# Ten scatters, then six: the row scatters of each batch split around the next inverse transform

## The reference, cut to what matters

```
u = x @ W_in + b_in
uc = _short_conv(u, short_w, short_b)          # three taps
x0, x1, v = split(uc, 3)
v = v * x1
v = _causal_fft_conv(v, k, filter_bias)        # k from a small sine network
y = v * x0
x = layernorm(x + y @ W_out + b_out)
probs = softmax(x @ gate_w.T);  top_w, top_idx = top_k(probs, 4)
act = silu(x @ w1) * (x @ w3);  eout = act @ w2          # for the 4 chosen experts
x = layernorm(x + sum(top_w * eout) + shared(x))
```

## Time and profile before

| | us |
|---|---|
| median of 3 runs | 703.61 |
| lowest, highest | 697.77, 704.76 |
| the profiled execution | 701.09 |
| its span in the trace | 699.3 |
| PE busy | 585.7 (84%) |
| DVE busy | 477.2 (68%) |
| ACT busy | 347.9 (50%) |
| POOL busy | 373.0 (53%) |

### The profile page before, as it was taken

The page is one execution under the profiler, slowest core; times in us unless marked ns, Lnnn a source line. Parts: engine busy times, 40 slices in busy tenths (PEclk is TensorE's granted clock), DMA queues, the critical chain, the costliest instruction groups (busy, mean ns, idle before and its releaser), DMA issues.

```text
span 699.3 us, 11663 instructions
## 1 busy us (share of the span) xinstructions
PE 585.7 (84%) x3264; PEld 504.2 (72%) x3265; DVE 477.2 (68%) x1108; ACT 347.9 (50%) x698; POOL 373.0 (53%) x341
## 2 busy tenths in 40 slices
PE   5795989989798997989857668898888999888853
PEld 3685868768587785877635568797787889788843
DVE  5869798949678696877956654444444459787835
ACT  3643456656367563666226134444444456465623
POOL 0535152756827568373647745554555547556561
PEclk9897999989899897998896589899999999999986
DMA  7395111633313232223847336664444488989756
GB/s 273 106 259 163 30 61 60 224 96 123 105 68 129 76 128 83 83 98 103 288 167 228 119 109 179 204 185 145 151 136 143 151 297 284 345 289 345 275 178 209
DMA packets 72369, 117.02 MB, mean 167 GB/s; under 512 B 10006, under 2 KB 54103, under 8 KB 72026
## 3 DMA queue, kind: packets, MB, share of 16 engines
q1 hardware_dynamic: 43114, 62.38, 28.8%
q0 software_dynamic: 21136, 45.76, 19.3%
q10 hardware_dynamic: 8080, 8.41, 3.4%
HBM read 72.86 MB, written 47.87 MB: 173 GB/s over the span
## 4 chain that ended last, share of the span: by engine, by line
PE 60%; DVE 15%; issue 11%; DMA 5%; ACT 3%; another core or an unknown queue 3%; SPq 2%; POOL 0%; ACTq 0%; DVEq 0%; POOLq 0%
PE bank L730 7%; PE bank L752 7%; PE bank L940 6%; PE bank L938 6%; PE bank L939 5%; PE bank L843 5%; PE bank L900 5%; PE bank L784 4%; PE bank L993 3%; PE bank L1026 3%; PE bank L892 3%; DMA row<-token_parts 2%; PE bank L909 2%; PE bank L964 2%
## 5 line engine op out<-in xcount | busy, mean ns | idle before, releaser
L689 POOL DMA_INDIRECT token_parts<-ty,goes x144 | 142.1, 987 | 122.9 <-issue 120.8
L674 POOL DMA_INDIRECT expert_rows<-row,slot x112 | 119.6, 1068 | 55.2 <-issue 31.7
L938 PE MATMUL bank<-w_hi,xtT_hi 128*128 x288 | 90.9, 316 | 8.4 <-DVE xtT_lo L1648 5.7
L1640 DVE SCALAR_TENSOR_TENSOR ta<-bank,xt,tsl 128x128 f32<-128x128 f32 x144 | 43.5, 343 | 62.8 <-ACT tsl L1199 43.5
L940 PE MATMUL bank<-w_hi,xtT_lo 128*128 x288 | 84.0, 292 | 1.0 <-issue 0.8
L939 PE MATMUL bank<-w_lo,xtT_hi 128*128 x288 | 84.0, 292 | 0.7 <-issue 0.5
L1199 ACT ACTIVATE tsl<-bank 128x256 f32<-128x256 f32 x72 | 28.7, 399 | 82.3 <-remote 39.7
L938 PEld LDWEIGHTS bank<-w_hi,xtT_hi 128*128 128x128 f32 x288 | 57.8, 201 | 12.7 <-issue 12.1
L1648 DVE TENSOR_TENSOR xtT_lo<-bank,xtT_hi 128x512 fp32r<-128x512 f32 x72 | 49.1, 683 | 20.3 <-issue 10.4
L843 PE MATMUL bank<-mats,Y 128*128 128x256 f32 x256 | 59.9, 393 | 2.2 <-DVE Y L1407 1.8
L1220 ACT COPY ty<-bank 128x512 f32<-128x512 f32 x72 | 43.7, 607 | 30.7 <-PE bank L940 15.8
(11 more groups left out here) (207 smaller groups left out, 1474.7 us busy)
## 6 DMA issues: line engine op xcount, KB each, us to landing
xt<-expert_rows SPq DMA_DIRECT2D x144, 129.0 KB
row<-token_parts SPq DMA_DIRECT2D x21, 640.0 KB
row_last<-token_parts SPq DMA_DIRECT2D x7, 640.0 KB
xT<-in_xT SPq DMA_DIRECT2D x8, 512.0 KB
xtok<-in_x SPq DMA_DIRECT2D x8, 512.0 KB, 3.5
w_hi<-in_w POOLq DMA_DIRECT2D x1, 4096.0 KB, 16.1
w_lo<-in_w SPq DMA_DIRECT2D x4, 1024.0 KB, 6.3
xT_hi<-in_xT POOLq DMA_DIRECT2D x7, 512.0 KB, 4.8
```

Source lines behind the costliest of these rows:

```text
L674: pool.indirect_dma_start(out=rows_d, out_offset=bass.IndirectOffsetOnAxis(ap=slot[q][:, n:n + 1], axis=0), in_=src[:, n // TOPK, n % TOPK ...
L689: pool.indirect_dma_start(out=parts_d, out_offset=bass.IndirectOffsetOnAxis(ap=goes[:, q_ * UNROLL + u:q_ * UNROLL + u + 1].bitcast(U32), ...
L938: te_.matmul(ps, x_hi, w_hi, start=first, stop=False)
L1640: ve.scalar_tensor_tensor(ta[:, v % 2, a, :], bank[2 + v % 2][:, (2 * a + 1) * HID:(2 * a + 2) * HID], xt[:, q_ * UNROLL + 2 * v + a, D:D ...
```

## The change

POOL's 16 scatters of a batch are divided into three groups, of 5, 5 and 6. For batches 0 to 5 the first ten are issued where the sixteen were, at the end of the body. The last six are issued in the next body, after the first half of x0's additions, and behind a wait for the second `pe_y` of that body, that is for the end of its inverse transform; the second half of x0, xT_lo and the bias come after them. For batch 6 the groups of five stand at the end of body 7 and behind the gate matmuls of body 8, the six behind its ranks. For batch 7 the second five wait for the first pair of expert tiles on PE (`t_h`), the six for the third pair. On ACT the square root now stands after two of the four row copies. The number of instructions that do work is unchanged on all engines.

```diff
--- before.py
+++ after.py
@@ -72,6 +72,7 @@
 NPART = 4
 PART = W13 // NPART
 LOW = 1024
+GROUPS = (range(5), range(5, 10), range(10, TT * TOPK))
 NPAD = (E + SPARE) * P
 EPS = 1e-5
 ROUND = 1.5 * 2.0 ** 23
@@ -626,9 +627,9 @@
                                         in1=bout[:, :].unsqueeze(1).broadcast_to([P, TT, D]),
                                         op=ALU.add).then_inc(pool_xb, 1)
 
-            def conv_x0(i, q):
-
-                for c in range(DC):
+            def conv_x0(i, q, halves=range(DC)):
+
+                for c in halves:
                     dst = x0[q][:, c, :]
                     pool.wait_ge(act_tap, 2 * DC * i + DC + c + 1)
                     nc.gpsimd.tensor_tensor(out=dst, in0=dst, in1=prodA[:, c, :], op=ALU.add).then_inc(pool_conv, 1)
@@ -650,8 +651,19 @@
                                    io["w2"].rearrange("e h d -> h e d")).then_inc(ld_moe, 16)
                 if two_next(i):
                     round_x(i + 2)
+                if not has_this(i):
+                    pool.wait_ge(pe_gate, i)
+                    scatters(i - 2, q, GROUPS[1])
                 if has_next(i):
-                    conv_x0(i + 1, 1 - q)
+                    conv_x0(i + 1, 1 - q, range(1))
+                if not (is0(i) or is1(i)):
+                    if has_this(i):
+                        pool.wait_ge(pe_y, DC * (i + 1))
+                    else:
+                        pool.wait_ge(pe_rank, i)
+                    scatters(i - 2, q, GROUPS[2])
+                if has_next(i):
+                    conv_x0(i + 1, 1 - q, range(1, DC))
                 if two_next(i):
                     rest_x(i + 2)
                 if has_next(i):
@@ -660,14 +672,19 @@
 
                     pool.wait_ge(dve_slot, SLOT_N * i)
                     pool.wait_ge(dve_row, 3 * i)
-                    late = isinstance(i, int) and i >= B - 1
-                    if not late:
+                    if not (isinstance(i, int) and i >= B - 1):
                         pool.wait_ge(act_row, TT * i)
                     pool.sem_inc(pool_seen, 1)
-                    for n in range(TT * TOPK):
-                        if late and n % TOPK == 0:
-                            pool.wait_ge(act_row, TT * (i - 1) + n // TOPK + 1)
-                        scatter(n, 1 - q, row_of(i - 1))
+                    scatters(i - 1, 1 - q, GROUPS[0])
+                    if not (isinstance(i, int) and i >= B - 1):
+                        scatters(i - 1, 1 - q, GROUPS[1])
+
+            def scatters(b, q, group):
+
+                for n in group:
+                    if isinstance(b, int) and b >= B - 2 and n % TOPK == 0:
+                        pool.wait_ge(act_row, TT * b + n // TOPK + 1)
+                    scatter(n, q, row_of(b))
 
             def scatter(n, q, src):
 
@@ -676,6 +693,9 @@
                     in_=src[:, n // TOPK, n % TOPK, :], in_offset=None).then_inc(scattered, 16)
 
             batches(pool, body, 3, B - 3)
+            for n in (1, 2):
+                pool.wait_ge(t_h, 2 * n - 1)
+                scatters(B - 1, (B - 1) % 2, GROUPS[n])
 
             def turn(g, j, q, h, *b):
                 pair = back(g, j, q, h, AT_Y)
@@ -1161,11 +1181,13 @@
                 if has_next(i):
                     copy_zT(i + 1)
                 if not is0(i) and has_next(i):
-                    fill_rows(i - 1, 1 - q)
+                    fill_rows(i - 1, 1 - q, range(TT // 2))
                 if has_this(i):
 
                     act.wait_ge(ln_var, i + 1)
                     sc.activation(sd[:, :], var[:, :], ACT.Sqrt).then_inc(ln_sd, 1)
+                if not is0(i) and has_next(i):
+                    fill_rows(i - 1, 1 - q, range(TT // 2, TT))
                 if is_end(i):
                     fill_rows(i - 1, 1 - q, range(1))
```

## The result

| | kernel before | changed kernel |
|---|---|---|
| median of the runs, us | 701.57 (4 runs, 697.77 to 704.76) | 671.31 (4 runs, 668.61 to 680.26) |
| profiled execution, us (span) | 701.09 (699.3) | 668.61 (666.7) |
| mean granted clock | 0.903 | 0.933 |

The ratio is 0.9554, with a 95% interval of 0.9504 to 0.9604: 4.5% faster. Medians hold all runs; ratios leave out the slow ones, which here is the run of 680.26 us. The forecast was 677 us, range 664 to 692.

What follows compares the result with a forecast made beforehand. It took PE's signals arriving late while POOL issues scatters to bound the batches. Gains of 23.7 + 1 + 1 = 25.7 us took the profiled 701.09 us to 675.4, quoted as 677 for the median, range 664 to 692.

Steps and rivals of the forecast that it cites:

- Point 1: Batches 2 to 6: sixteen scatters in a row become ten and six; gain 23.7 us, between 19.6 and 28.2.
- hold-up: While POOL issues a long row of scatters, work that waits for PE starts late; batches average 42.73 us, batch 1 37.10.
- the hold-up moves: Rival, 30%: the six scatters delay signals of L900, z's transposes and the output projection; 40.0 us a batch, 687 us.
- No effect: Rival, 8%: PE's transform ends late for reasons of its own, only small shifts are left; 701 us, 697 to 706.
- Point 2: First half of x0's additions ahead of the six: 0 to 2.6 us on DVE per batch; what follows them costs nothing.
- Point 3: ACT's square root between the row copies: cost 0; two copies, 1.95 us, no longer stand ahead of it.
- the slack I counted on: ACT's cover in batch 3, from the last row copy's end at about 202.8 to the next scatter at 206.77.
- Point 4: Batch 7 and the last part: a gain of 1 us each, bounds gain 4 to loss 4 each.

Runs made afterwards that it cites:

- e4: The changed kernel without POOL's wait for the inverse transform ahead of the six scatters; 676.97 us, ratio 0.9609 to the kernel before.
- e3: The changed kernel with both halves of x0's additions behind the six scatters; 675.70 us, ratio 0.9664 to the kernel before.
- t1: The changed kernel with 16 scatters in one row again in the batches, keeping the new last part; 605.97 us against 606.62 for the kernel before.
- c1: The changed kernel itself, unedited, on a chip without the hold-up; 618.06 us against 604.62 for the kernel before, ratio 1.0247.
- x1: The kernel before with 16 scatters of 128 pieces of 8 bytes added at the head of batch 1; 603.82 us beside 604.62.
- x2: The kernel of x1 once more, on another chip; 603.79 us beside 605.98 for the kernel before.
- r1: The changed kernel with 13 scatters, the wait for the transform, three scatters, then both halves of x0's additions; 607.04 us against 605.98 for the kernel before.
- t2: The changed kernel with its scatters grouped 13 and 3 instead of ten and six; 614.66 us, ratio 1.0118 to the kernel before.
- e1: The kernel before with only ACT's square root moved between the second and third row copy; 699.42 us against 701.64.
- e2: The changed kernel with the square root back behind all four row copies; 674.50 us, ratio 0.9643 to the kernel before.

## Why the prediction was right, and what it did not see

**Point 1, right, and its cause has two witnesses.** Forecast 23.7 us, measured 24.75, from the places named: yx, the gates, the clock. The witnesses for the row of scatters as the cause are e4 (the idle returns in batch 7 when the pause is taken out) and e3 (a pause with no additions in it frees the gates and yx of batch 3 as well). t1 adds that the undivided row runs at 35.64 us a batch where signals are not held. With t1 and c1 as the levels without a hold-up, the batches can be taken apart, across chips and from one profiled execution each. The old order lost 213.66 - 178.20 = 35.5 us to the hold-up. The new one loses 188.91 - 187.30 = 1.6. So the change removed 33.9 us and cost 187.30 - 178.20 = 9.1 us of its own; the net is the 24.75. These parts are an estimate. t1 is not quite the old order, since it has the moved root; x1 and x2, the old order with 16 small scatters in batch 1, take 180.9 and 180.8 us for the same five stretches, and by them the change removed about 31 and cost about 6.5. My sum arrived close to the net partly by luck: it had neither the full saving nor the full cost. Its floor was wrong too. I took batch 1's 37.10 us as the least a batch can take, and two stretches of the changed kernel took 36.86 and 36.60 us on the same kind of chip, t1's 35.6.

**The rival "the hold-up moves".** Its signs showed small: DVE's second r waits 2.38 us in batch 3, 3.5 us in all five. It did not reach the 2 to 3 us a batch that its 687 needed. "No effect" is refused where the kernel before takes 701 us. The sentence of the Trainium skill behind it ("SBUF — State Buffer", section "Who interferes with whom", PE and ACT never wait on anyone) is about the ports of SBUF, and no run here shows a port as the cause of the hold-up. Read as I read it, that scatters leave PE and its signals untouched, it does not hold there (the 4.12 us of e4); on the chips of t1, c1 and r1 the traces agree with it (gates in 1.85 us).

**Point 2, right for the first half, mis-sized for the rest.** The collision came where I put it, at 0 to 2.6 us a batch; in batch 3 z alone paid 1.96. But I costed what comes behind the six at nothing, because PE needs xT_lo late. I did not ask what DVE does beside it. On the first chip xT_lo and the bias fall on the norm, whose operations of 0.15 us last 1.66 and 2.26 us, and PE waits 6.4 us for the slots. The kernel before paid one such collision a batch, 2.17 us for nmr in batch 3. On c1's chip the norm of batch 3 is untouched; the conv operations and onehot are hit, and the wait for aT is 6.8 of the 9.1 us. The half ahead is nearly by itself in r1 against t2: 177.90 and 186.60 us for the five batches, so 8.7 us, 1.7 a batch, within my bounds, though from two chips. What xT_lo and the bias cost on the first chip no run has by itself.

**Point 3, right in size.** e1 and e2 show no cost or gain that can be measured. I also wrote that the place matters because copies would wait for later scatters. The copies do wait (14.8 us), so the slack I counted on is gone, yet in e2 DVE stood for the root only 2.2 us in five batches, and the batches took no longer than with the moved root.

**Point 4, 2 us forecast, 7.8 measured.** In batch 7 the pause saved the second yx 3.2 us, as the 4.12 of e4 against 0.91 shows; the start of the expert stage has the rest of the 3.4 us up to the first token scatter. The other 4.4 us are not explained. e2, with the same code behind batch 6 but for the root in batch 7, took 362.8 us for what took the profiled change 357.12, so a difference of this size may lie between executions. I also quoted 677 where 675.4 and 2.5 give 677.9. On a chip without the hold-up the new last part is worth nothing (t1).

**What no step had.** I read the hold-up as a property of the kernel alone; it also needs something that one of four chips had when it was used. I found nothing in the profile of one chip that tells. Batch 1, without scatters, looked the same on both: its gates took 1.85 us in x1 too.

**Left open.** What makes a chip hold PE's signals; whether the issue of descriptors or their traffic does it (x1 and x2 missed such a chip); r1 on such a chip. In the last part the changed kernel still takes 357.12 us there against 308.60 on c1's chip. Those 48.5 us, more than the batches ever lost, are beyond what this change reaches. They carry the same sign. In the expert stage of the changed kernel on the first chip the list of waits has

```profile
ACT tsl L1221 <- remote: 26.4, 5, 6.1
```

and POOL's own scatters stand 111.9 us in "issue"; in c1 no wait has a releaser that is not on record, and POOL's stand 62.4. This points to the hold-up in the expert stage too, but no run tested it.

## What to carry to other kernels

When an engine idles although its releaser ended long before, ask whether it is the program or the chip, and time both orders on more than one chip before keeping the new one: here the same change is 4.5% faster on one and 2.5% slower on another. Where signals wait for the end of a long row of scatters, a break in the row frees them; that a break is free of cost elsewhere is not shown. Before moving vector work on POOL, look at what DVE has beside it, small operations of a chain above all.

## What the runs showed of the hardware

- The kernel before took 701.6 us on the chip of e1 to e4 and 606.6, 604.6 and 606.0 us on three others. With the old order the five batches took 213.66 us on a chip of the first kind and 178.20 on one of the second, and all behind them 364.97 us before the change and 304.20 in t1.
- A scatter of 128 pieces takes POOL 1.14 us at 8 bytes a piece (x1) and 1.04 to 1.07 at 1032 bytes (the kernel before, the changed kernel, t1): the bytes do not set its price.
- A DVE operation on 128x4 elements, 0.15 us by itself, lasted up to 2.32 us beside a POOL operation on 128x1024, until that one ended (e3: 188.52 to 190.84 beside 188.46 to 190.82).
- In a row of 16 scatters on the first chip the 16 gate matmuls, with no wait between them, took from 179.75 to 187.2 us; in t1 and in batch 1 they took 1.85.
